# A GRU recurrence followed by a routed spline: the spline's program moves into the recurrence's block, and the last tile's work changes its order

## The chip, the cores and the metric

The kernel runs on one core of one Trainium2 chip. The metric is the device time of one execution in microseconds, median of three. Times inside an execution are counted from the start of the span, which runs from the first instruction to the last.

## What is computed

The reference, cut to what matters:

```python
xs = jnp.swapaxes(inputs, 0, 1)                  # a GRU over 1024 steps, batch 4, width 1024
_, hs = jax.lax.scan(cell, initial_state, xs)
xn = layernorm(hs) * ln_gamma + ln_beta          # 4096 tokens of 1024
...                                              # signs of xn choose one of 64 experts for each token
x_slice = 16 consecutive elements of xn, those of the token's expert
mn, mx = least and greatest element of x_slice over all tokens of the same expert
u = clip((x_slice - mn) / (mx - mn + 1e-8), 0, 1 - 1e-6)
gi = (u * 16) as an integer
delta = (bases[expert, j, gi] + slopes[expert, j, gi] * local) * output_scale[expert]
y = x + hs + delta, which is added at the 16 elements only
```

The extremes of an expert need all the tokens. So the last part, the spline, can start only when the last tile of tokens has been routed.

## The kernel before, in words

The program is a row of blocks. In a block each engine has an instruction stream of its own; at the end of a block every engine executes a DRAIN and waits in a barrier for the others (these instructions bear the line of the `with nc.Block()`: 145, 566, 1399). The third block, at line 566, holds the recurrence, the fourth, at line 1399, the spline.

The recurrence works in tiles of 128 tokens (two time steps of 64 chains); there are 32. While tile i is computed, the tile before is normalised and the tile before that is routed. For one tile this goes: SP loads the states (`h_tok`, L1226); ScalarE sums and squares them (`act_sum`, `act_squares`, L725 to L731); GpSimd makes `rstd` and `shift` (`pool_scale`, L1099 to L1103); ScalarE normalises (`act_normalise`, L735); VectorE applies gamma and beta (`dve_signed`, L893, L895); ScalarE takes the signs (L740); VectorE scores the experts (`dve_route`, L910 to L922), which gives `hit` and `tile_id`; GpSimd keeps them and gathers the token's 16 elements (`pool_keep`, L1115 to L1124, a DMA that GpSimd issues), then copies them (`pool_pick`, L1131). GpSimd also issues, for each tile, the DMA that adds the states to y (`pool_add`, L1110). The extremes are gathered in three batches, `dve_ends(p, batch, part)`: batch 1 is 12 tiles, batch 2 the last two. Part 0 (L949 to L956) needs the picks, part 1 (L958 to L960) makes `miss`, parts 2 and 3 (L962 to L968) fold into `ends`.

The helper `passes` writes each engine's program as: the body once; a wait for `flag`; a load of `flag` into a register (L559); a branch that skips a second copy of the body with a loop around it. With these inputs the branch is taken on every engine. SP waits at L1340 for the last `pool_add` (`y_added`).

The spline: TensorE turns `ends` (L1404) and then computes `curves(0)`, 12 matmuls that look up the curves of the first four tiles (L1413). VectorE reduces the turned ends and splits them into `row_parts` (L1442 to L1445, with L404 to L408 as helper); TensorE looks up each token's extremes (`per_token`, L1420); VectorE computes the cells (L1457 to L1474) and chooses among curves (`choose`, L1484 to L1490). For each group of three or four tiles GpSimd then issues one indirect DMA for a tile, 32 in all (L1503), which add `delta` to y; it waits for all of them at the end.

Of the kernel before, what the change touches and what calls it, by code (L numbers as in the profile page):

```python
# [13 lines left out]
P = 128  # L14
# [396 lines left out]
def recurrence(nc, ctx, t, h0, gi_dram, sums_dram, states_dram, hs_dram, x_rows, y_rows, tables, late_w):  # L411
# [3 lines left out]

    def pb(name, shape, dt=F32):
        return ctx.enter_context(nc.psum_tensor(name, shape, dt))
# [73 lines left out]

    rz_bank = [pb(f"rz_bank{s}", [P, 512]) for s in range(SETS)]
    n_bank = [pb(f"n_bank{s}", [P, 512]) for s in range(SETS)]
    hit_bank = pb("hit_bank", [P, 512])
    misc_bank = pb("misc_bank", [P, 512])
    affine = pb("affine", [P, TILES, 2 * SLICE])
    affine_banks = affine[:].rearrange("p i f -> p (i f)")
    late_acc = [hit_bank[:], misc_bank[:], affine_banks[:, 0:512], affine_banks[:, 512:1024]]
# [67 lines left out]
    with nc.Block() as block:  # L566
# [75 lines left out]
        def _(pe):  # L642
# [43 lines left out]
            passes(pe, one_pass)  # L686

        def act_step(act, it, u, s, turns, mode=FULL, after_gates=None, after_tanh=None):
            n = steps_to(it, u)
            if mode == DIFFS:  # L690
                act.wait_ge(rz_done[s], n)
                nc.scalar.activation(rz[:, s], rz_bank[s][:], ACT.Sigmoid, scale=UNSCALE).then_inc(rz_ready[s], 1)
# [130 lines left out]
        def dve_step(dve, it, u, s, seeds, mode=FULL, after_sums=None, after_old=None):  # L823
# [7 lines left out]
            else:  # L831
                dve.wait_ge(rz_done[s], n)
                dve.wait_ge(gi_loaded[s][u], it * 64 + 64)
                nc.vector.scalar_tensor_tensor(out=sums[:, s, 0:RZ], in0=rz_bank[s][:], scalar=UNSCALE, in1=gi[:, s, u, 0:RZ],  # L834
# [136 lines left out]
        def _(dve):  # L971
# [50 lines left out]
            def one_pass(p, first):  # L1022
# [71 lines left out]
            passes(dve, one_pass)  # L1094

# [38 lines left out]
        def _(pool):  # L1134
# [22 lines left out]
            def one_pass(p, first):  # L1157
# [190 lines left out]
def spline(nc, ctx, t, y_slices):  # L1348

    def sb(name, shape, dt=F32):  # L1350
        return ctx.enter_context(nc.sbuf_tensor(name, shape, dt))
# [33 lines left out]
    tok_bank = ctx.enter_context(nc.psum_tensor("tok_bank", [P, 512], F32))  # L1385
    turn_bank = tok_bank[0:NT, 4 * TILES:4 * TILES + 2 * P]
    curve_bank = ctx.enter_context(nc.psum_tensor("curve_bank", [P, 7, 512], F32))
# [3 lines left out]
    math_step, delta_ready, added = (sem(n) for n in ("math_step", "delta_ready", "added"))  # L1391
# [7 lines left out]
    with nc.Block() as block:  # L1399

        @block.tensor
        def _(pe):
            for e in range(2):
                ins = nc.tensor.transpose(turn_bank[:, e * P:(e + 1) * P], t["ends"][:, e], t["ident"][:])  # L1404
            ins.then_inc(ends_turned, 1)

            def curves(g):
                if g >= 2:
                    pe.wait_ge(curve_used, g - 1)
                a, b = GROUPS[g]  # L1410
                for i in range(a, b):
                    for part in range(3):
                        ins = nc.tensor.matmul(curve_bank[:, 4 * (g % 2) + i - a], hits_t[:, i], curve_parts[:, part],  # L1413
                                               start=part == 0, stop=part == 2)
                ins.then_inc(curve_ready, 1)

            def per_token(a, b):
                for i in range(a, b):
                    for part in range(3):
                        ins = nc.tensor.matmul(tok_bank[:, i * 4:(i + 1) * 4], hits_t[:, i], row_parts[:, part],  # L1420
                                               start=part == 0, stop=part == 2)
                ins.then_inc(tok_ready, 1)

            curves(0)
            pe.wait_ge(rows_split, 1)
            per_token(*CELLS[0])
            pe.wait_ge(tok_known, 1)
            per_token(CELLS[0][1], TILES)
            for g in range(1, len(GROUPS)):
                curves(g)  # L1430

        @block.vector
        def _(dve):
            done = [0]

            def step(ins):
                done[0] += 1
                ins.then_inc(math_step, 1)
                dve.wait_ge(math_step, done[0])

            dve.wait_ge(ends_turned, 1)
            step(nc.vector.tensor_reduce(rows[:, ROW_EXT:ROW_EXT + 1], turn_bank[:, 0:P], AX.X, ALU.min))  # L1442
            step(nc.vector.tensor_reduce(rows[:, ROW_EXT + 1:ROW], turn_bank[:, P:2 * P], AX.X, ALU.max))
            split_exactly(nc.vector, dve, [row_parts[:, i] for i in range(3)], [row_left[:, i] for i in range(2)],
                          rows[:, ROW_SCALE:ROW], step).then_inc(rows_split, 1)  # L1445

            def wide(ap):
                return ap.rearrange("p (i o) -> p i o", o=1).broadcast_to([P, ap.shape[1], SLICE])

            def cells(n):  # L1450
                a, b = CELLS[n]
                s = slice(a, b)
                scale, tile_id, low, high = (per_tok[:, s, f] for f in range(4))
                if n < 2:
                    known = slice(a, TILES if n else b)
                    dve.wait_ge(tok_ready, n + 1)
                    nc.vector.tensor_copy(per_tok[:, known], tok_bank[:, 4 * a:4 * known.stop].rearrange("p (i f) -> p i f", f=4))                      .then_inc(tok_known, 1)  # L1457
                    dve.wait_ge(tok_known, n + 1)
                step(nc.vector.tensor_tensor(span[:, s], high, low, ALU.subtract))
                step(nc.vector.tensor_scalar(span_eps[:, s], span[:, s], 1e-8, None, ALU.add))  # L1460
                step(nc.vector.tensor_tensor(off[:, s], records[:, s], wide(low), ALU.subtract))  # L1461
                step(nc.vector.reciprocal(rspan[:, s], span_eps[:, s]))
                step(nc.vector.tensor_tensor(u_raw[:, s], off[:, s], wide(rspan[:, s]), ALU.mult))  # L1463
                step(nc.vector.tensor_scalar(u_clip[:, s], u_raw[:, s], 0.0, 1.0 - 1e-6, ALU.max, ALU.min))  # L1464
                step(nc.vector.tensor_scalar(u_grid[:, s], u_clip[:, s], float(GRID), None, ALU.mult))  # L1465

                step(nc.vector.tensor_copy(near_i[:, s], u_grid[:, s]))  # L1467
                step(nc.vector.tensor_copy(near[:, s], near_i[:, s]))  # L1468
                step(nc.vector.tensor_tensor(above[:, s], near[:, s], u_grid[:, s], ALU.is_gt))  # L1469
                step(nc.vector.tensor_tensor(cell[:, s], near[:, s], above[:, s], ALU.subtract))  # L1470
                step(nc.vector.tensor_copy(cell_i[:, s], cell[:, s]))  # L1471
                for k, half in enumerate(HALVES):
                    nc.vector.tensor_scalar(in_upper[:, k, s], cell_i[:, s], half, None, ALU.bitwise_and)  # L1473
                step(nc.vector.tensor_tensor(local[:, s], u_grid[:, s], cell[:, s], ALU.subtract))  # L1474

            def choose(g):

                a, b = GROUPS[g]
                s = slice(a, b)
                curve = curves_of(g)  # L1480
                dve.wait_ge(curve_ready, g + 1)
                for k, half in enumerate(HALVES):
                    upper = in_upper[:, k, s].rearrange("p i j -> p (i j)").rearrange("p (m c g) -> p m c g", c=1, g=1)
                    step(nc.vector.copy_predicated(curve[:, :, :, 0:half], upper.broadcast_to([P, (b - a) * SLICE, 2, half]),  # L1484
                                                   curve[:, :, :, half:2 * half]))
                base, slope = (curve[:, :, c, 0].rearrange("p (i j) -> p i j", j=SLICE) for c in range(2))
# [5 lines left out]
            for n, (a, b) in enumerate(CELLS):  # L1492
                cells(n)
                for g, (first, last) in enumerate(GROUPS):
                    if a <= first < b:
                        choose(g)
# [121 lines left out]
```

## Time and profile before

| what | value |
|---|---|
| median of three runs | 2510.69 us (2509.69 to 2511.22) |
| profiled execution, its own time | 2510.37 us |
| its span | 2508.6 us |
| TensorE busy | 2354.8 us (94%) |
| VectorE busy | 1301.2 us (52%) |
| ScalarE busy | 661.4 us (26%) |
| GpSimd busy | 190.5 us (8%) |
| mean granted TensorE clock | 0.965 |

The profiled execution takes 1.8 us more than its span. TensorE's share is an average over three stages: the last 110 us or so, where the last tile is finished and the spline runs, look quite different from the rest. A profile reader should look at that tail by its timeline, with the instructions of the sequencers (load, branch, drain) that do not count as busy.

### The profile page before, as it was taken

How to read it: one execution, taken by the hardware profiler on the slowest of the kernel's cores; microseconds unless marked ns; L12 is line 12 of the kernel's file. 1: busy time of each engine (PE TensorE's matmuls, PEld its weight loads, DVE VectorE, ACT ScalarE, POOL GpSimd, SP SyncE). 2: the span in 40 equal slices, each digit the busy share in tenths (PEclk: the TensorE clock that was granted, in tenths of full speed). 3: DMA queues.
4: the chain of work that ended last, by engine and by line, in shares of the span. 5: the costliest groups of instructions: out<-in, count | busy, mean ns of one | idle time of the engine just before them, and what ended most of it. 6: DMA issues, size and time to landing. Idle time of an engine off the chain costs nothing. (4 is left out here: it accounts for less than half of the span.)

```text
span 2508.6 us, 83678 instructions
## 1 busy us (share of the span) xinstructions
PE 2354.8 (94%) x35300; PEld 1294.4 (52%) x35300; DVE 1301.2 (52%) x2682; ACT 661.4 (26%) x1333; POOL 190.5 (8%) x376
## 2 busy tenths in 40 slices
PE   7999999999999989999999999999999999977734
PEld 3444444444444444555666666666666666544411
DVE  4322121212123357676666655666666666888865
ACT  2200000000001223333333333333333333355510
POOL 0000000000000000000000000111111111122217
PEclk9999999999999999999999999999999999999955
DMA  6594131313132455443444444444444444477712
GB/s 213 166 345 163 51 126 51 126 52 129 51 143 101 151 156 153 138 150 116 136 135 135 135 127 111 118 117 117 117 116 117 115 116 119 128 228 233 219 43 4
DMA packets 179894, 330.33 MB, mean 132 GB/s; under 512 B 27856, under 2 KB 89728, under 8 KB 178752
## 3 DMA queue, kind: packets, MB, share of 16 engines
q1 hardware_dynamic: 145360, 267.53, 33.7%
q10 hardware_dynamic: 24192, 44.05, 4.7%
q0 software_dynamic: 10240, 17.31, 4.7%
q8 instruction: 75, 1.23, 0.2%
q14 instruction: 27, 0.22, 0.0%
HBM read 222.13 MB, written 156.77 MB: 151 GB/s over the span
## 5 line engine op out<-in xcount | busy, mean ns | idle before, releaser
L573 PE MATMUL rz_bank<-w_hi,hi 128*32 128x512 f16 x6912 | 422.7, 387 | 52.9 <-DVE hi L869 36.7
L308 DVE SCALAR_TENSOR_TENSOR out_stage<-acc,bias_row 128x512 f32<-128x512 f32 x168 | 116.2, 691 | 629.0 <-PE acc L364 629.0
L362 PE MATMUL acc<-w_hi,x_even 128*128 128x512 f16 x768 | 293.3, 382 | 17.8 <-DVE x_even L300 11.3
L573 PEld LDWEIGHTS rz_bank<-w_hi,hi 128*32 128x32 f16 x6912 | 177.9, 98 | 231.6 <-DVE hi L869 44.8
L363 PE MATMUL acc<-w_hi,x_even 128*128 128x512 f16 x768 | 293.1, 382 | 0.0
L364 PE MATMUL acc<-w_lo,x_even 128*128 128x512 f16 x768 | 292.9, 381 | 0.0
L696 ACT ACTIVATE rz<-sums 128x512 f32<-128x512 f32 x176 | 111.1, 631 | 541.2 <-DVE sums L834 540.9
L834 DVE SCALAR_TENSOR_TENSOR sums<-rz_bank,stage 128x512 f32<-128x512 f32 x176 | 121.5, 690 | 244.9 <-PE rz_bank L573 244.8
L573 PE MATMUL rz_bank<-w_lo,hi 128*32 128x512 f16 x4096 | 243.4, 379 | 0.0
L573 PE MATMUL rz_bank<-w_hi,lo 128*32 128x512 f16 x4096 | 243.4, 379 | 0.0
L573 PE MATMUL n_bank<-w_hi,hi 128*32 128x256 f16 x6912 | 234.8, 279 | 0.0
L573 PEld LDWEIGHTS n_bank<-w_hi,hi 128*32 128x32 f16 x6912 | 191.3, 100 | 55.5 <-issue 5.9
L362 PE MATMUL acc<-w_hi,x_keep 128*128 128x512 f16 x576 | 218.3, 379 | 0.4 <-issue 0.4
L363 PE MATMUL acc<-w_hi,x_keep 128*128 128x512 f16 x576 | 218.3, 379 | 0.0
L364 PE MATMUL acc<-w_lo,x_keep 128*128 128x512 f16 x576 | 218.3, 379 | 0.0
L573 PEld LDWEIGHTS rz_bank<-w_hi,lo 128*32 128x32 f16 x4096 | 111.2, 97 | 82.7
L573 PEld LDWEIGHTS rz_bank<-w_lo,hi 128*32 128x32 f16 x4096 | 111.1, 97 | 82.8 <-issue 0.2
L701 ACT ACTIVATE n_act<-n_sum 128x256 f32<-128x256 f32 x216 | 90.3, 418 | 179.0 <-DVE n_sum L847 178.3
L573 PE MATMUL n_bank<-w_hi,lo 128*32 128x256 f16 x4096 | 134.2, 273 | 0.0
L573 PE MATMUL n_bank<-w_lo,hi 128*32 128x256 f16 x4096 | 134.2, 273 | 0.0
L362 PEld LDWEIGHTS acc<-w_hi,x_even 128*128 128x128 f16 x768 | 75.5, 98 | 109.9 <-issue 13.6
L573 PEld LDWEIGHTS n_bank<-w_hi,lo 128*32 128x32 f16 x4096 | 110.2, 97 | 28.9
(191 smaller groups left out, 2665.3 us busy)
## 6 DMA issues: line engine op xcount, KB each, us to landing
stage<-gi_scratch SPq DMA_DIRECT2D x704, 96.0 KB
gi_scratch<-out_stage ACTq DMA_DIRECT2D x168, 256.0 KB, 2.0
stage<-sums_scratch SPq DMA_DIRECT2D x40, 512.0 KB
stage<-in_xT SPq DMA_DIRECT2D x32, 512.0 KB, 6.4
y<-in_x_rows SPq DMA_DIRECT2D x32, 512.0 KB, 4.4
hs_scratch<-h SPq DMA_DIRECT2D x128, 128.0 KB
x_keep<-hs_scratch SPq DMA_DIRECT2D x32, 512.0 KB, 3.9
y<-hs_scratch POOLq DMA_DIRECT2D x32, 512.0 KB
```

The lines of the kernel that those rows point to most:

```text
L308: nc.vector.scalar_tensor_tensor(out=out_stage[:, tb], in0=acc[e % BANKS][:], scalar=UNSCALE, in1=bias_row[:].rearrange("p q f -> p (q f)" ...
L362: nc.tensor.matmul(acc[e % BANKS][:], hi, wh, start=k == 0, stop=False)
L363: nc.tensor.matmul(acc[e % BANKS][:], lo, wh, start=False, stop=False)
L364: last = nc.tensor.matmul(acc[e % BANKS][:], hi, wl, start=False, stop=k == KB - 1)
L573: last = nc.tensor.matmul(bank[q * COLS:(q + 1) * COLS, 0:b - a], state[:, s, j], w[:, j, q * QW + a:q * QW + b], start=first and j == 0, ...
L696: nc.scalar.activation(rz[:, s], sums[:, s, 0:RZ], ACT.Sigmoid).then_inc(rz_ready[s], 1)
L701: nc.scalar.activation(n_act[:, s], n_sum[:, s], ACT.Tanh).then_inc(n_ready[s], 1)
L834: nc.vector.scalar_tensor_tensor(out=sums[:, s, 0:RZ], in0=rz_bank[s][:], scalar=UNSCALE, in1=gi[:, s, u, 0:RZ], op0=ALU.mult, op1=ALU.add ...
```

## The change

The spline no longer has a block of its own. `spline()` returns three functions, for TensorE, VectorE and GpSimd, and the recurrence calls each behind `passes` in the same block. In them `curves(0)` comes ahead of the turning of `ends`; a semaphore `ends_ready`, which VectorE increments at the start of its part, stands where the barrier stood. The PSUM banks are one tensor for both parts, and the spline's scratch lies in the room of `w_lo`. GpSimd waits for `y_added` as well, behind its last pick. The loop over tiles on GpSimd ends one tile earlier and the last turn is written out: keep, scale, add, pick, where it was add, keep, scale, pick. On VectorE part 1 of batch 1 comes ahead of `dve_signed`.

```diff
@@ def one_pass (VectorE)
                 nc.vector.tensor_copy(flag[:], misc_bank[0:1, 64:65]).then_inc(pass_judged, 1)
+                dve_ends(dve, p, 1, 1)
                 dve_signed(dve, T)
-                dve_ends(dve, p, 1, 1)
                 dve_route(dve, T)
@@
             passes(dve, one_pass)
+            dve_spline(dve)
@@ def one_pass (GpSimd)
-                with pool.Fori(2, TILES + 1) as i:
+                with pool.Fori(2, TILES) as i:
                     tile(i, True)
+                T = p * TILES + TILES
+                pool_keep(pool, T - 1, TILES - 2)
+                pool_scale(pool, T, TILES - 1)
+                pool_add(pool, T, TILES - 1)
+                pool_pick(pool, T - 1, TILES - 2)
                 pool_keep(pool, p * TILES + TILES, TILES - 1)
                 pool_pick(pool, p * TILES + TILES, TILES - 1)
+                pool.wait_ge(y_added, p * (TILES * 16) + TILES * 16)
+                pool.sem_inc(wait_carrier, 1)
 
             passes(pool, one_pass)
+            pool_spline(pool)
@@ spline
-    with nc.Block() as block:
-        @block.tensor
-        def _(pe):
-            for e in range(2):
-                ins = nc.tensor.transpose(turn_bank[:, e * P:(e + 1) * P], t["ends"][:, e], t["ident"][:])
-            ins.then_inc(ends_turned, 1)
...
-            curves(0)
-            pe.wait_ge(rows_split, 1)
+    def pe_spline(pe):
...
+        curves(0)
+        pe.wait_ge(ends_ready, 1)
+        for e in range(2):
+            ins = nc.tensor.transpose(turn_bank[:, e * P:(e + 1) * P], t["ends"][:, e], t["ident"][:])
+        ins.then_inc(ends_turned, 1)
+        pe.wait_ge(rows_split, 1)
...
+    def dve_spline(dve):
...
+        dve.sem_inc(ends_ready, 1)
+        dve.wait_ge(ends_turned, 1)
```

## Rows read from the trace of the kernel before

**Rows 1.** The page, busy time of each engine over the whole span.

```profile
PE 2354.8 (94%) x35300; PEld 1294.4 (52%) x35300; DVE 1301.2 (52%) x2682; ACT 661.4 (26%) x1333; POOL 190.5 (8%) x376
```

**Rows 2.** The chain that ended last, in order of time: start, us, what.

```profile
2429.90 0.61 PE tok_bank L1404 x2
2430.50 5.23 PE curve_bank L1413 x12
2435.73 0.31 PE tok_bank L1420 x12
...
2436.07 0.19 DVE per_tok L1457
...
2502.42 1.55 POOL y L1503
```

**Rows 3.** The timeline from 2398 to 2444 us: start, us, engine, line, idle time before.

```profile
2398.27 0.08 DVE L922 DVE_READ_ACCUMULATOR late_out<-late_out,best,tile_ids 128x1 f32 x1
...
2400.48 1.00 POOL L1110 DMA_DIRECT2D y<-hs_scratch  x1 [11.16 <-DMA x_keep<-hs_scratch]
...
2402.13 0.19 ACT L731 ACTIVATION_READ_ACCUMULATOR x_keep<-x_keep,neg_mean 128x1 f32 x1
...
2403.08 1.11 POOL L1124 DMA_INDIRECT late_out<-hs_scratch,row_now  x1 [0.71 <-ACT x_keep L731]
2404.26 0.19 POOL L1099 TENSOR_SCALAR var_eps<-square_sum 128x1 f32<-128x1 f32 x1
...
2405.59 1.24 ACT L735 ACTIVATE x_keep<-x_keep,shift,rstd 128x1024 f32<-128x1024 f32 x1 [3.27 <-POOL shift L1103]
...
2406.86 1.23 DVE L893 TENSOR_TENSOR x_keep<-x_keep,gamma_s 128x1024 f32<-128x1024 f32 x1 [3.14 <-ACT x_keep L735]
...
2409.26 0.55 DVE L958 TENSOR_SCALAR late_out<-bias_row 128x768 f32<-128x768 bf16 x1
2409.38 1.06 ACT L740 ACTIVATE bias_row<-x_keep 128x1024 bf16<-128x1024 f32 x1 [2.39 <-DVE x_keep L895]
...
2411.84 1.22 DVE L910 TENSOR_REDUCE late_out<-bias_row 128x64 f32<-128x1024 bf16 x1
...
2420.36 0.19 DVE L949 TENSOR_TENSOR late_out<-picks,rstd 128x32 f32<-128x32 f32 x1 [0.45 <-POOL picks L1131]
...
2424.31 0.23 DVE L968 TENSOR_TENSOR ends<-late_out,ends 128x64 f32<-128x64 f32 x1
...
2431.94 0.16 DVE L408 CAST row_parts<-row_left 64x4 bf16<-64x4 f32 x1
...
2443.57 1.65 POOL L1503 DMA_INDIRECT y<-delta,row_i  x1 [23.40 <-DVE delta L1490]
```

**Rows 4.** Line 559, load of the flag and branch: ns min/median/max, first and last start.

```profile
L559 PEldq COMPARE_BRANCH  x1: 3698/3698/3698, 2416.4 to 2416.4; - x1
...
L559 DVEq TENSOR_LOAD <-flag x1: 548/548/548, 2424.7 to 2424.7; - x1
...
L559 DVEq COMPARE_BRANCH  x1: 56/56/56, 2426.0 to 2426.0; - x1
```

**Rows 5.** Line 566, the end of the recurrence's block.

```profile
L566 POOLq DRAIN  x1: 5297/5297/5297, 2421.0 to 2421.0; - x1
L566 DVEq DRAIN  x1: 77/77/77, 2429.5 to 2429.5; - x1
```

**Rows 6.** Line 1399, the end of the spline's block.

```profile
L1399 POOLq DRAIN  x1: 2660/2660/2660, 2505.7 to 2505.7; - x1
```

**Rows 7.** Line 145, the end of the second block.

```profile
L145 POOLq DRAIN  x1: 41/41/41, 3.3 to 3.3; - x1
```

**Rows 8.** The three lines on which GpSimd issues DMAs, each asked for alone.

```profile
L1110 POOL DMA_DIRECT2D y<-hs_scratch x32: 894/992/1101, 1528.7 to 2400.5; - x32
L1124 POOL DMA_INDIRECT late_out<-hs_scratch,row_now x32: 1081/1102/1177, 1572.9 to 2416.1; - x32
L1503 POOL DMA_INDIRECT y<-delta,row_i x32: 1545/1554/1653, 2443.6 to 2502.4; - x32
```

More of the change, by code:

```diff
@@ L1 @@
+import math
 import concourse.bass as bass
@@ L490, in recurrence @@
     rstd, shift, hits_t = t["rstd"], t["shift"], t["hits_t"]
[L492 to L498, printed above, removed]
+    banks = t["banks"]
+    rz_bank = [banks[:, s] for s in range(SETS)]
+    n_bank = [banks[:, SETS + s] for s in range(SETS)]
+    hit_bank, misc_bank = banks[:, 4], banks[:, 5]
+    affine = banks[:, 6:8].rearrange("p b f -> p (b f)").rearrange("p (i f) -> p i f", f=2 * SLICE)
+    late_acc = [banks[:, 4 + tb] for tb in range(TB)]
     gi_loaded = t["gi_loaded"]
@@ L1348, in spline @@
 def spline(nc, ctx, t, y_slices):
+    room = t["w_lo"][:].rearrange("p k n -> p (k n)")
+    taken = [0]
     def sb(name, shape, dt=F32):
-        return ctx.enter_context(nc.sbuf_tensor(name, shape, dt))
+        halves = math.prod(shape[1:]) * (1 if dt == BF16 else 2)
+        flat = room[0:shape[0], taken[0]:taken[0] + halves].bitcast(dt)
+        taken[0] += (halves + 15) // 16 * 16
+        dims = "abc"[:len(shape) - 1]
+        return flat.rearrange(f"p ({' '.join(dims)}) -> p {' '.join(dims)}", **dict(zip(dims, shape[1:])))
     def sem(name):
@@ L1384, in spline @@
     CELLS = ((0, 4), (4, 18), (18, TILES))
-    tok_bank = ctx.enter_context(nc.psum_tensor("tok_bank", [P, 512], F32))
+    tok_bank = t["banks"][:, 7]
     turn_bank = tok_bank[0:NT, 4 * TILES:4 * TILES + 2 * P]
-    curve_bank = ctx.enter_context(nc.psum_tensor("curve_bank", [P, 7, 512], F32))
+    curve_bank = t["banks"][:, 0:7]
     ends_turned, row_step, rows_split, tok_ready, tok_known, curve_ready, curve_used = (
         sem(n) for n in ("ends_turned", "row_step", "rows_split2", "tok_ready", "tok_known", "curve_ready", "curve_used"))
-    math_step, delta_ready, added = (sem(n) for n in ("math_step", "delta_ready", "added"))
+    math_step, delta_ready, added, ends_ready = (sem(n) for n in ("math_step", "delta_ready", "added", "ends_ready"))
     def curves_of(g):
@@ L1397, in curves_of @@
         return curve_bank[:, first:first + b - a].rearrange("p i (j c g) -> p (i j) c g", c=2, g=GRID)
-    with nc.Block() as block:
-        @block.tensor
-        def _(pe):
-            for e in range(2):
-                ins = nc.tensor.transpose(turn_bank[:, e * P:(e + 1) * P], t["ends"][:, e], t["ident"][:])
-            ins.then_inc(ends_turned, 1)
[L1407 to L1422, printed above, removed]
-            curves(0)
-            pe.wait_ge(rows_split, 1)
[L1426 to L1486, printed above, removed]
-                step(nc.vector.tensor_tensor(rise[:, s], slope, local[:, s], ALU.mult))
-                nc.vector.tensor_tensor(value[:, s], base, rise[:, s], ALU.add).then_inc(curve_used, 1)
-                dve.wait_ge(curve_used, g + 1)
-                nc.vector.tensor_tensor(delta[:, s], value[:, s], wide(per_tok[:, s, 0]), ALU.mult).then_inc(delta_ready, 1)
[L1492 to L1496, printed above, removed]
-        @block.gpsimd
-        def _(pool):
-            for g, (a, b) in enumerate(GROUPS):
-                pool.wait_ge(delta_ready, g + 1)
-                for i in range(a, b):
-                    pool.indirect_dma_start(out=y_slices[:], out_offset=bass.IndirectOffsetOnAxis(ap=row_i[:, i:i + 1], axis=0),
-                                            in_=delta[:, i], in_offset=None, compute_op=ALU.add).then_inc(added, 16)
-            pool.wait_ge(added, 16 * TILES)
@@ new lines, in pe_spline, with curves, per_token @@
+    def pe_spline(pe):
+        def curves(g):
+            if g >= 2:
+                pe.wait_ge(curve_used, g - 1)
+            a, b = GROUPS[g]
+            for i in range(a, b):
+                for part in range(3):
+                    ins = nc.tensor.matmul(curve_bank[:, 4 * (g % 2) + i - a], hits_t[:, i], curve_parts[:, part],
+                                           start=part == 0, stop=part == 2)
+            ins.then_inc(curve_ready, 1)
+        def per_token(a, b):
+            for i in range(a, b):
+                for part in range(3):
+                    ins = nc.tensor.matmul(tok_bank[:, i * 4:(i + 1) * 4], hits_t[:, i], row_parts[:, part],
+                                           start=part == 0, stop=part == 2)
+            ins.then_inc(tok_ready, 1)
+        curves(0)
[4 more added lines that the diff above has]
+        pe.wait_ge(rows_split, 1)
+        per_token(*CELLS[0])
+        pe.wait_ge(tok_known, 1)
+        per_token(CELLS[0][1], TILES)
+        for g in range(1, len(GROUPS)):
+            curves(g)
@@ new lines, in dve_spline, with step, wide, cells @@
+    def dve_spline(dve):
+        done = [0]
+        def step(ins):
+            done[0] += 1
+            ins.then_inc(math_step, 1)
+            dve.wait_ge(math_step, done[0])
+        dve.sem_inc(ends_ready, 1)
+        dve.wait_ge(ends_turned, 1)
+        step(nc.vector.tensor_reduce(rows[:, ROW_EXT:ROW_EXT + 1], turn_bank[:, 0:P], AX.X, ALU.min))
+        step(nc.vector.tensor_reduce(rows[:, ROW_EXT + 1:ROW], turn_bank[:, P:2 * P], AX.X, ALU.max))
+        split_exactly(nc.vector, dve, [row_parts[:, i] for i in range(3)], [row_left[:, i] for i in range(2)],
+                      rows[:, ROW_SCALE:ROW], step).then_inc(rows_split, 1)
+        def wide(ap):
+            return ap.rearrange("p (i o) -> p i o", o=1).broadcast_to([P, ap.shape[1], SLICE])
+        def cells(n):
+            a, b = CELLS[n]
+            s = slice(a, b)
+            scale, tile_id, low, high = (per_tok[:, s, f] for f in range(4))
+            if n < 2:
+                known = slice(a, TILES if n else b)
+                dve.wait_ge(tok_ready, n + 1)
+                nc.vector.tensor_copy(per_tok[:, known], tok_bank[:, 4 * a:4 * known.stop].rearrange("p (i f) -> p i f", f=4))                      .then_inc(tok_known, 1)
+                dve.wait_ge(tok_known, n + 1)
+            step(nc.vector.tensor_tensor(span[:, s], high, low, ALU.subtract))
+            step(nc.vector.tensor_scalar(span_eps[:, s], span[:, s], 1e-8, None, ALU.add))
+            step(nc.vector.tensor_tensor(off[:, s], records[:, s], wide(low), ALU.subtract))
+            step(nc.vector.reciprocal(rspan[:, s], span_eps[:, s]))
+            step(nc.vector.tensor_tensor(u_raw[:, s], off[:, s], wide(rspan[:, s]), ALU.mult))
+            step(nc.vector.tensor_scalar(u_clip[:, s], u_raw[:, s], 0.0, 1.0 - 1e-6, ALU.max, ALU.min))
+            step(nc.vector.tensor_scalar(u_grid[:, s], u_clip[:, s], float(GRID), None, ALU.mult))
+            step(nc.vector.tensor_copy(near_i[:, s], u_grid[:, s]))
+            step(nc.vector.tensor_copy(near[:, s], near_i[:, s]))
+            step(nc.vector.tensor_tensor(above[:, s], near[:, s], u_grid[:, s], ALU.is_gt))
+            step(nc.vector.tensor_tensor(cell[:, s], near[:, s], above[:, s], ALU.subtract))
+            step(nc.vector.tensor_copy(cell_i[:, s], cell[:, s]))
+            for k, half in enumerate(HALVES):
+                nc.vector.tensor_scalar(in_upper[:, k, s], cell_i[:, s], half, None, ALU.bitwise_and)
+            step(nc.vector.tensor_tensor(local[:, s], u_grid[:, s], cell[:, s], ALU.subtract))
+        def choose(g):
+            a, b = GROUPS[g]
+            s = slice(a, b)
+            curve = curves_of(g)
+            dve.wait_ge(curve_ready, g + 1)
+            for k, half in enumerate(HALVES):
+                upper = in_upper[:, k, s].rearrange("p i j -> p (i j)").rearrange("p (m c g) -> p m c g", c=1, g=1)
+                step(nc.vector.copy_predicated(curve[:, :, :, 0:half], upper.broadcast_to([P, (b - a) * SLICE, 2, half]),
+                                               curve[:, :, :, half:2 * half]))
+            base, slope = (curve[:, :, c, 0].rearrange("p (i j) -> p i j", j=SLICE) for c in range(2))
+            step(nc.vector.tensor_tensor(rise[:, s], slope, local[:, s], ALU.mult))
+            nc.vector.tensor_tensor(value[:, s], base, rise[:, s], ALU.add).then_inc(curve_used, 1)
+            dve.wait_ge(curve_used, g + 1)
+            nc.vector.tensor_tensor(delta[:, s], value[:, s], wide(per_tok[:, s, 0]), ALU.mult).then_inc(delta_ready, 1)
+        for n, (a, b) in enumerate(CELLS):
+            cells(n)
+            for g, (first, last) in enumerate(GROUPS):
+                if a <= first < b:
+                    choose(g)
@@ L1508, in constants, with pool_spline @@
+    def pool_spline(pool):
+        for g, (a, b) in enumerate(GROUPS):
+            pool.wait_ge(delta_ready, g + 1)
+            for i in range(a, b):
+                pool.indirect_dma_start(out=y_slices[:], out_offset=bass.IndirectOffsetOnAxis(ap=row_i[:, i:i + 1], axis=0),
+                                        in_=delta[:, i], in_offset=None, compute_op=ALU.add).then_inc(added, 16)
+        pool.wait_ge(added, 16 * TILES)
+    return pe_spline, dve_spline, pool_spline
 def constants(nc, t):
```

14 lines of the change are left out of this document (6 added, 8 removed).

## The prediction

> **What bounds the kernel now.** I read the page first. TensorE is busy 94% of the span [rows 1], but that is the recurrence, which the change leaves alone: no instruction of its loops is added, removed or moved, apart from GpSimd's last turn. So I looked at the end. The chain in order of time [rows 2] shows what sets it from 2430 us on: the two transposes, `curves(0)` for 5.23 us, `per_token`, VectorE's cells, and then GpSimd's indirect DMAs, the last of which is issued at 2502.42. The reader is to see that the first `curves(0)` stands between the transposes and `per_token`. Then I read the timeline of the 30 us ahead of it, to follow the last tile from engine to engine [rows 3], and last the sequencers' own instructions at lines 559, 566, 1399 and 145 [rows 4 to 7], since a barrier and a branch are not busy time and the timeline leaves them out. All of 2398 to 2508 us is one thread of short waits, so a microsecond saved in it comes off the end, unless something takes it back behind it.
>
> **The last tile's order.** Two moves, of which both must hold for the gain.
>
> GpSimd: before, it waits for the states' load, issues `pool_add` at 2400.48, keeps, issues the gather at 2403.08 (1.11 us), and only at 2404.26 starts `pool_scale`, though the sum of squares was there at 2402.13 + 0.19 = 2402.32 [rows 3]. After, keep needs only `tile_id`, there at 2398.35 (2398.27 + 0.08), and can start then. From 2400.48 to the end of the gather's issue at 2404.19 it took 3.7 us with the add inside, 2.7 without it. So GpSimd is free at about 2401.1 and scale starts near 2402.45, when it is the squares that come last. Scale takes 2405.59 - 2404.26 = 1.33 us to ScalarE's start, so `xhat` starts at 2403.8 and is done at 2405.0, against 2406.83: 1.8 us earlier. `pool_add` comes behind it with 1.0 us of GpSimd; the pick, the next keep and SP's wait stand behind it, and the next keep is not due for 7 us.
>
> VectorE: the flag is copied at 2406.86 - 3.14 = 2403.72, then it idles until `xhat`. Part 1 of batch 1 takes 2411.84 - 2409.26 = 2.58 us and fits from 2403.74 to 2406.3. `dve_signed` then starts at 2406.3; it takes 2.49 us (2406.86 to 2409.35), ScalarE's signs 1.06 and two handovers of 0.03. Routing starts at 2409.9 against 2411.84 [rows 3]: **1.9 us saved**. The cover is gone that part 1 gave to the signs: VectorE now idles 1.1 us there, which is counted in it. Had GpSimd's part gained nothing, `dve_signed` would start at 2406.86 still and 1.4 us would be left. Behind routing the order stands: keep, gather, pick, with parts 2 and 3 beside them, which leave 0.45 us of idle before L949 in both. So `ends` are finished at 2424.54 - 1.9 = 2422.6. The lower bound of this term is 1.4, the upper 2.0.
>
> **The barrier.** From the end of `ends` at 2424.54 to the transposes at 2429.90 lie 5.3 us, and the idle time looks like the barrier's. It isn't. VectorE loads the flag at 2424.7 (0.55 us), reaches its branch at 2426.0, and its first instruction behind the branch, the DRAIN, is at 2429.5 [rows 4, 5]; TensorE's branch took 3.7 us in the same way. The code to be skipped is as long after the change, VectorE's `ends_ready` stands behind the same branch, and it is TensorE that waits for it. So 5.0 of the 5.3 us stay. What goes is the barrier's own handshake, 2429.5 to 2429.9; a semaphore of about 0.15 us takes its place. **0.2 us saved**, between 0 and 0.35.
>
> **`curves(0)` ahead.** TensorE's branch at 2416.4 lands 3.7 us later [rows 4], at 2418.2 with the 1.9 taken off; 5.2 us of `curves(0)` end at 2423.5, where `ends_ready` comes at 2427.6. So it lies under VectorE's branch with 4 us to spare. If that cover were gone it would cost up to 5.2. Then `row_parts`, done at 2432.10 (2431.94 + 0.16), let `per_token` start at once. Its 12 small matmuls added 0.31 us behind a full TensorE, and two transposes took 0.61 from a standstill [rows 2]; I take 0.55 for them and 0.1 for the handover. The copy that stood at 2436.07 would stand at 2432.75: **3.3 us saved**, between 3.2 and 3.6. From `per_token` on every distance is as before: cells, choose, first scatter 7.5 us later, 32 scatters. GpSimd's added wait for `y_added` is met by 2410 or so, while it would scatter at 2438.1.
>
> Sum so far: 1.9 + 0.2 + 3.3 = 5.4 us. The last scatter is issued at 2497.0 and landed at 2500.1, not 2505.5.
>
> **The DRAIN at the end.** This is where I expect the gain to go. GpSimd's DRAIN at the end of the recurrence took 5.30 us, from 2421.0 to 2426.3, under VectorE's branch, so that nobody waited for it [rows 5]. Its DRAIN at the end of the spline took 2.66 us, and it ends the span [rows 6]. Neither waits for a transfer: the pick had landed before the first, and the second stands behind the wait for all 32 scatters. Where GpSimd had issued no DMA, the DRAIN took 0.04 us [rows 7]. Now count: 32 adds and 32 gathers stand ahead of the first DRAIN, 32 scatters ahead of the second [rows 8]. 5.297 / 64 is 0.083 us for a DMA; 2.660 / 32 is 0.083 us. I read it as work that GpSimd owes for each DMA it has issued since the last DRAIN. With one block there is one DRAIN, behind all 96: 96 x 0.083 = 7.96 us, at the end, where nothing covers it. That is **5.3 us lost**. Any cost that adds up over DMAs gives the same, whatever share each kind has. The bounds: 0 if the length doesn't go by what was issued (then 2.66 stays), 5.3 if it adds up. I take 5.3, because two rows and the empty one lie on a line through nothing.
>
> The Trainium skill, VectorE: DVE Perf Modes, section "The DRAIN you can't avoid", calls the DRAINs that surround a kernel boilerplate of a constant 12 ns or so on all engines. By that page the merged DRAIN would cost nothing more, and the time would be 2505.3. These rows (5.297 and 2.660 us on GpSimd) already speak against it here.
>
> **The sum** against the profiled execution (2510.37 us, its span of 2508.6 and 1.8 around it): 2510.37 - 5.4 + 5.3 = 2510.3. The median of the runs, 2510.69, is 0.3 above the profiled one; against it I get 2510.6 and take **2510.5 us**.
>
> **Rivals.**
>
> 1. The DRAIN is no longer than before (2.66 us), be it constant or reset in another way. For it: a DRAIN that starts after all has landed has nothing obvious to do. Against it: rows 5 to 7. It gives 2510.7 - 5.4 = 2505.3 us, faster by 0.21%, just over the bound.
> 2. The DRAIN's debt has a ceiling, at the 64 DMAs seen: 5.3 us in place of 2.66. For it: nothing longer was seen. Against it: nothing shows a ceiling either. It gives 2510.7 - 5.4 + 2.6 = 2507.9.
> 3. Slower: the debt grows faster than the count when 96 DMAs stand before one DRAIN. The place is the same last DRAIN. To make the kernel slower by 0.2% (5.0 us) it must take 2.66 + 5.4 + 5.0 = 13.1 us, or 0.136 us for a DMA; at 0.15 the DRAIN is 14.4 and the time 2517.0. Against it: from 32 to 64 the price for one stayed 0.083.
> 4. The order doesn't do what it says: VectorE still waits for `xhat`, or the gather lands later. Then up to 1.9 us of the gain are missing, and with the DRAIN of 7.96 the time is 2512.4, still within the bound.
>
> A measurement of this kernel can tell about 0.2%, 5.0 us, from no change.
>
> **How the numbers follow.** Chances: my forecast 0.64; rival 1 0.16; rival 2 0.08; rival 3 0.04; rival 4 0.08. Rival 1 lies on the edge of the bound, so about two thirds of it count as faster, and a few hundredths for gains I missed: faster 0.13. Slower is rival 3 and a little for what I don't see: 0.05. The rest, 0.82, is within. The range takes in the forecast, rivals 2 and 4 and the spread of the runs shown (1.5 us): 2507.0 to 2512.8. It leaves out rivals 1 and 3, which hold 2 in 10.
>
> **What would show it.** In the profile after: routing of the last tile starts about 1.9 us earlier relative to the load of the states; `ends` to transposes stays near 5.1 us, with some 3.5 of it behind VectorE's branch; `curves(0)` ends some 4 us before the transposes; `per_token` follows `row_parts` in 0.1 us; the last scatter is issued near 2497.0. The step that decides is the one GpSimd DRAIN at the end of line 566: near 8.0 us by my reading, 2.7 by rival 1, 5.3 by rival 2. The prediction is wrong if that DRAIN is short, or if VectorE's branch lands sooner when no barrier stands behind it, which would give up to 3.5 us more.

## The result, and the profile after

The kernel after takes 2506.91 us (median of 20 runs, 2505.1 to 2509.56) against 2510.61 us before (20 runs): 3.7 us less, a ratio of 0.9984 with a 95% interval of 0.9977 to 0.9991. I had said 2510.5 us, 2507.0 to 2512.8. So the time moved where I had forecast no change that could be told, and it lies just under my range. The profiled execution took 2506.94 us, its span 2505.4 us against 2508.6.

First the timeline after, for the stretch of [rows 3]: the last tile.

```profile
2399.85 1.07 POOL L1124 DMA_INDIRECT late_out<-hs_scratch,row_now  x1 [0.57 <-issue]
...
2402.49 0.18 POOL L1099 TENSOR_SCALAR var_eps<-square_sum 128x1 f32<-128x1 f32 x1 [1.57 <-ACT x_keep L730]
...
2403.57 0.54 DVE L957 TENSOR_SCALAR late_out<-bias_row 128x768 f32<-128x768 bf16 x1
2403.64 1.24 ACT L734 ACTIVATE x_keep<-x_keep,shift,rstd 128x1024 f32<-128x1024 f32 x1 [1.34 <-POOL shift L1103]
2404.00 1.01 POOL L1110 DMA_DIRECT2D y<-hs_scratch  x1 [0.40 <-issue]
...
2406.16 1.23 DVE L892 TENSOR_TENSOR x_keep<-x_keep,gamma_s 128x1024 f32<-128x1024 f32 x1
...
2409.77 1.22 DVE L909 TENSOR_REDUCE late_out<-bias_row 128x64 f32<-128x1024 bf16 x1 [1.12 <-ACT bias_row L739]
...
2418.21 5.30 PE L1421 MATMUL banks<-curve_parts,late_ring 64*128 64x512 bf16 x12 [4.60 <-issue]
...
2422.33 0.22 DVE L967 TENSOR_TENSOR ends<-late_out,ends 128x64 f32<-128x64 f32 x1
...
2437.93 1.62 POOL L1514 DMA_INDIRECT y<-w_lo,row_i  x1 [19.74 <-DVE w_lo L1502]
```

GpSimd's scale now waits for ScalarE's squares (1.57 us idle ahead of L1099), where before the squares had lain ready from 2402.32 until GpSimd took them up at 2404.26. `miss` (L957) starts at once behind the flag, and `signed` (L892) behind it without idle time. Routing (L909) starts at 2409.77 against 2411.84 [rows 3]. `curves(0)` (L1421) is done at 2423.5, well ahead of the turning of `ends`.

The chain in order of time, for the stretch of [rows 2]:

```profile
2424.00 0.06 DVEq L557
2424.05 3.50 issue
2427.56 0.03 DVEq L1452
2427.59 0.04 issue
2427.63 0.65 PE banks L1435 x2
...
2429.93 0.49 PE banks L1428 x12
2430.44 0.18 DVE w_lo L1469
```

With the barrier gone the profile names what [rows 4, 5] showed between the lines: from VectorE's branch (line 557 now) to its next instruction, the increment of `ends_ready` (L1452), 3.50 us pass in which it waits for nothing that the profile shows. Then the turning of `ends` and `per_token` follow at once.

And the end of the block (line 564 now), which answers to [rows 5, 6]:

```profile
L564 POOLq DRAIN  x1: 5338/5338/5338, 2499.8 to 2499.8; - x1
```

That is the surprise. The one DRAIN behind 96 DMAs takes 5.34 us: more than the 2.66 before, less than the 7.96 that I had added up.

### The profile page after: what moved, and what is told of

It is laid out like the page before. It is cut to its first block and busy times, and to the rows that moved or that the text cites. A ratio compares the mean times of both kernels' runs of the same rounds, so it can differ in the third digit from the quotient of the medians.

```text
span 2505.4 us, 83655 instructions
## 1 busy us (share of the span) xinstructions
PE 2339.9 (93%) x35300; PEld 1288.7 (51%) x35300; DVE 1299.7 (52%) x2682; ACT 660.6 (26%) x1333; POOL 189.4 (8%) x376
## 5 line engine op out<-in xcount | busy, mean ns | idle before, releaser
L571 PE MATMUL banks<-w_hi,hi 128*32 128x512 f16 (+1 forms) x13824 | 605.1, 328 | 61.4 <-DVE hi L868 45.3
L571 PEld LDWEIGHTS banks<-w_hi,hi 128*32 128x32 f16 x13824 | 363.3, 97 | 288.3 <-DVE hi L868 56.2
L571 PE MATMUL banks<-w_hi,lo 128*32 128x512 f16 (+1 forms) x8192 | 355.2, 326 | 0.0
L571 PE MATMUL banks<-w_lo,hi 128*32 128x512 f16 (+1 forms) x8192 | 355.2, 326 | 0.0
L571 PEld LDWEIGHTS banks<-w_lo,hi 128*32 128x32 f16 x8192 | 221.3, 97 | 111.7
L571 PEld LDWEIGHTS banks<-w_hi,lo 128*32 128x32 f16 x8192 | 221.2, 97 | 111.7
L833 DVE SCALAR_TENSOR_TENSOR sums<-banks,stage 128x512 f32<-128x512 f32 x176 | 121.3, 689 | 247.6 <-PE banks L571 247.5
L364 PEld LDWEIGHTS acc<-w_hi,x_even 128*128 128x128 f16 x768 | 75.5, 98 | 109.6 <-issue 12.9
L366 PEld LDWEIGHTS acc<-w_lo,x_even 128*128 128x128 f16 x768 | 75.5, 98 | 91.8 <-issue 2.1
L365 PEld LDWEIGHTS acc<-w_hi,x_even 128*128 128x128 f16 x768 | 75.5, 98 | 91.3 <-issue 1.7
L858 DVE TENSOR_TENSOR n_sum<-not_z,n_act 128x256 f32<-128x256 f32 x216 | 91.5, 423 | 36.9 <-ACT n_act L700 36.9
```

Source lines behind the costliest of these rows:

```text
L364: nc.tensor.matmul(acc[e % BANKS][:], hi, wh, start=k == 0, stop=False)
L365: nc.tensor.matmul(acc[e % BANKS][:], lo, wh, start=False, stop=False)
L366: last = nc.tensor.matmul(acc[e % BANKS][:], hi, wl, start=False, stop=k == KB - 1)
L571: last = nc.tensor.matmul(bank[q * COLS:(q + 1) * COLS, 0:b - a], state[:, s, j], w[:, j, q * QW + a:q * QW + b], start=first and j == 0, ...
L858: nc.vector.tensor_tensor(new_n[:, s], not_z[:, s], n_act[:, s], ALU.mult).then_inc(new_n_ready[s], 1)
```

## The experiments

All medians stand against the kernel before on the same chip (2510.57 us, 2510.87 for the second set, which is experiments 2 and 7 to 9, and one run of 2510.19 in experiment 3). The time of one kernel varies by 4 to 6 us from run to run (2509.14 to 2514.53 before, 2505.10 to 2509.56 after). In the profiled runs of the kernels with the new order the last tile but one is kept on GpSimd (L1115 in the kernel after) anywhere from 2396.95 to 2403.07 us, so much of this lies ahead of the tail. So I read a small part from distances inside the tail.

**1. What a DRAIN of GpSimd costs.** A kernel of blocks. In each, GpSimd issues n DMAs of one kind, waits for them (every 32, and at the end), and the block ends:

```python
for i in range(n):
    issue(pool, kind, i, sem)
    if i % 32 == 31:
        pool.wait_ge(sem, 16 * (i + 1))
pool.wait_ge(sem, 16 * n)
```

> A kernel of blocks in which only GpSimd issues DMAs, waits for all of them, and ends the block with its DRAIN; it computes nothing of the reference. Theory 1 (bookkeeping of 0.083 us for each DMA since the last DRAIN, with a ceiling at about 64): gathers of 128 rows, 8, 16, 32, 48, 64, 80, 96 and 128 of them, give DRAINs of 0.7, 1.3, 2.7, 4.0, 5.3, 5.3, 5.3 and 5.3 us; 32, 64 and 96 scatters 2.7, 5.3 and 5.3; 32 adds of 128 KB, 32 loads and 32 tiny loads of one row 2.7 each, 96 of them 5.3; one tiny load 0.1. Theory 2 (the work goes by descriptors, and the ceiling is that of a descriptor ring): tiny loads of one row give far less than gathers of 128 rows, 32 tiny ones under 0.5 us, 96 of them about three times as much, with no ceiling there. Theory 3 (the adds and the gathers of the recurrence cost, and the scatters beside them do not, or the other way): gathers and scatters of the same number give different DRAINs, and each kind grows in a straight line with its number.

Measured, the GpSimd row of each block's line:

```profile
L59 POOLq DRAIN  x1: 2655/2655/2655, 133.0 to 133.0; - x1
...
L63 POOLq DRAIN  x1: 5268/5268/5268, 287.2 to 287.2; - x1
...
L67 POOLq DRAIN  x1: 7882/7882/7882, 529.7 to 529.7; - x1
...
L69 POOLq DRAIN  x1: 1262/1262/1262, 707.3 to 707.3; - x1
...
L71 POOLq DRAIN  x1: 2655/2655/2655, 770.4 to 770.4; - x1
...
L73 POOLq DRAIN  x1: 2817/2817/2817, 897.2 to 897.2; - x1
...
L75 POOLq DRAIN  x1: 5432/5432/5432, 1084.8 to 1084.8; - x1
...
L85 POOLq DRAIN  x1: 7877/7877/7877, 1279.8 to 1279.8; - x1
```

These are 32, 64, 96 and 128 gathers, then 32, 64 and 96 scatters, and last 96 loads of 64 bytes. 8, 16, 48 and 80 gathers gave 0.72, 1.35, 3.96 and 6.57 us; 32 adds 2.66, 32 loads 2.65, one load of 64 bytes 0.12. From 8 to 96 gathers the DRAIN rises by (7.882 - 0.719) / 88 = 0.081 us for each, and 96 loads of one row cost the same as 96 gathers of 128 rows. So the price goes by the number of DMAs and not by their kind, size or descriptors, and with that theories 2 and 3 fall as to the price. But the ceiling of theory 1 falls too: 96 gathers cost 7.9 us. Instead the length drops: 128 gathers leave the debt of about 15, 64 scatters that of 34, 96 scatters that of 66. I call what is owed for one DMA an entry, and read the drop as entries that were cleared before the DRAIN came. The timeline shows a place for it, where an issue waits for nothing that the profile shows and yet comes late:

```profile
687.11 0.95 POOL L20 DMA_INDIRECT room<-in_x,rows  x1 [3.13 <-issue]
...
888.28 1.55 POOL L23 DMA_INDIRECT y<-room,rows  x1 [1.78 <-issue]
```

The first is the 114th of the 128 gathers, the second the 61st of the 64 scatters; elsewhere this idle time is 0.30 us. When the clearing comes does depend on the kind.

**2. The same with the recurrence's own mixture**, 32 adds of 512 KB and 32 gathers in turn, and then 0 to 64 scatters.

> A kernel of blocks in which only GpSimd issues DMAs and ends each with its DRAIN; it computes nothing of the reference. Each of the first eight begins as the recurrence does (32 adds of 512 KB and 32 gathers in turn, each waited for) and goes on with 0, 4, 8, 12, 16, 24, 32 and 64 scatters. Theory A (an entry is owed for every DMA, 0.082 us each in the DRAIN, and when some store of them is full, entries are cleared in the stream of issues): the DRAIN rises by 0.082 us for each scatter from 5.3 us, falls by about 2.5 us (31 entries) at one number of scatters between 4 and 32, where the interval between two issues is longer by 1 to 1.5 us, and stands at 5.3 us again with 32 scatters. Theory B (a ceiling of 64 or 65 entries): 5.3 us for every number of scatters, with no drop and no long interval. In the blocks of one kind theory A expects: 48 scatters 4.0, 62 scatters 2.7, 112 gathers 9.2, 120 gathers 0.6 to 0.7; theory B expects nothing of the kind, as the first ladder already had 7.9 us for 96 gathers.

```profile
L61 POOLq DRAIN  x1: 5290/5290/5290, 315.2 to 315.2; - x1
...
L65 POOLq DRAIN  x1: 5926/5926/5926, 878.2 to 878.2; - x1
...
L67 POOLq DRAIN  x1: 3190/3190/3190, 1171.5 to 1171.5; - x1
...
L73 POOLq DRAIN  x1: 4823/4823/4823, 2113.0 to 2113.0; - x1
```

These are the blocks with 0, 8, 12 and 32 scatters. Between 8 and 12 the DRAIN falls by 2.7 us, where four more DMAs should add 0.3: some 37 entries went (3.06 us at 0.082 for each). The timeline of the block with 12 scatters shows the place, ahead of the last one:

```profile
1162.98 1.56 POOL L28 DMA_INDIRECT y<-room,rows  x1 [0.30 <-issue]
1164.85 1.56 POOL L28 DMA_INDIRECT y<-room,rows  x1 [0.30 <-issue]
1168.27 1.56 POOL L28 DMA_INDIRECT y<-room,rows  x1 [1.86 <-issue]
```

The idle time ahead of an issue is 1.86 us in place of 0.30. The blocks with 16, 24 and 32 scatters (3.52, 4.17 and 4.82 us) have the long idle time in the same place, ahead of the 76th DMA (1.84 to 1.88 us), and the blocks with 0, 4 and 8 have none. So theory A holds in its course up to 32 scatters: a rise of 0.08 for each, one drop, and a longer interval there; theory B, a ceiling, would have shown neither. Its numbers held less well: with 32 scatters I expected 5.3 us and got 4.8. In the blocks of one kind 48 and 62 scatters gave 3.96 and 2.66 us, 112 and 120 gathers 9.19 and 0.61, all as expected.

The blocks for which nothing was expected show that no single count sets the clearing. 64 scatters behind the mixture give 2.82 us, with long idle times ahead of the 76th and again the 114th DMA. 128 and 192 scatters (0.98 and 3.76 us) have them ahead of the 61st, the 114th and the 121st, and 192 also ahead of the 181st. 192 gathers (6.59 us) have one, ahead of the 114th; 192 loads of 64 bytes (5.27 us) have one of 4.52 us, ahead of the 129th; 32 gathers and 32 scatters in turn (5.27 us) have none.

**3. Where in the kernel after the entries go.** Three kernels with one more DRAIN, behind the 4th, 11th or 25th scatter. The edit of the first; the others have `i == 10` and `i == 24`:

```diff
                                         in_=delta[:, i], in_offset=None, compute_op=ALU.add).then_inc(added, 16)
+                if i == 3:
+                    pool.drain()
```

> The kernel after with one more DRAIN on GpSimd behind the 4th of the 32 scatters, where it waits for the second group in any case. It asks how many entries stand after 68 DMAs. With 0.0817 us for each entry and 0.05 on top: 68 entries give 5.6 us; if the 31 that are missing at the end (65 stand there and not 96) were cleared by then, 37 entries give 3.1. The last DRAIN then has 28 entries, 2.3 us.

> The same behind the 11th scatter, 75 DMAs in: 6.2 us if all 75 stand, 3.6 if 31 were cleared by then (the ladder with the same mixture cleared about 37 between the 75th and the 76th DMA, so 6.2 is the likelier). The last DRAIN has 21 entries, 1.8 us. Both DRAINs take about 0.25 us for the start as well, and the scatters behind it are later by its length.

> The same behind the 25th scatter, 89 DMAs in: 7.3 us if the clearing comes only at the very end, 4.8 if it came between the 12th and the 25th, as in the ladder. The last DRAIN has 7 entries, 0.6 us.

The rows of the three added DRAINs:

```profile
L1517 POOLq DRAIN  x1: 13085/13085/13085, 2436.2 to 2436.2; - x1
...
L1517 POOLq DRAIN  x1: 15710/15710/15710, 2452.2 to 2452.2; - x1
...
L1517 POOLq DRAIN  x1: 19922/19922/19922, 2468.8 to 2468.8; - x1
```

The first begins at 2436.2, ahead of the first scatter (2436.45), though it stands behind the 4th: such a row holds more than the DRAIN's work. So I count from the end of the issue ahead of it to its end. The first ends at 2449.30, and the issue ahead of it ended at 2443.66: 5.6 us, all 68 entries. Behind the 11th scatter the same distance is 6.2 us, all 75. Behind the 25th it is 5.0 us, and 89 entries would be 7.3: some 28 had gone. The last DRAINs, with 28, 21 and 7 scatters behind, took 2.34, 1.76 and 0.62 us, as expected. So in the kernel, too, entries are cleared on the way, behind the 11th scatter and by the 25th. What stays open: no interval in that stretch is longer by 1.5 us as it was in experiment 2 (from the first to the last issue 58.79 us pass in the kernel after, with the clearing, and as many in the kernel of experiment 4, whose last DRAIN shows none); why some 28 had gone at the 25th scatter and 31 at the end; and why 37 went in experiment 2. One time each was taken: 2508.01, 2512.63 and 2506.17 us, too few to rank these kernels. But a DRAIN between scatters is in their way: the idle time ahead of the next issue is 6.72, 6.93 and 5.76 us, where it was 1.31, 0.30 and 0.30.

**4. A DRAIN under cover.** The kernel after with one more DRAIN where GpSimd has nothing to do:

```diff
             passes(pool, one_pass)
+            pool.drain()
             pool_spline(pool)
```

> The kernel after, with one more DRAIN on GpSimd, behind the last pick and the flag's branch and ahead of the scatters. If the last DRAIN is long because of the 64 DMAs of the recurrence (theories 1 and 2), the new one takes 5.3 us from about 2419.2 to 2424.5, under VectorE's branch and ahead of the first scatter at 2437.9, and the last one falls from 5.34 to 2.66 us: span 2.7 us shorter than the kernel after, 2504.2 us against 2506.9. If the last DRAIN has a length that does not go by what was issued, it stays at 5.3 and so does the time, 2506.9.

```profile
L564 POOLq DRAIN  x1: 2660/2660/2660, 2499.7 to 2499.7; - x1
L1182 POOLq DRAIN  x1: 5297/5297/5297, 2418.9 to 2418.9; - x1
```

2504.89 us (10 runs), ratio 0.9978 (0.9968 to 0.9987); the span of the profiled run is 2502.6 us, 2.8 less than after. (The medians differ by 2.0 us and their intervals overlap, so the rows and the span carry this reading.) The second row is the new one, at 2418.9 to 2424.2, and the first scatter comes at 2437.7 as before. The merge had moved 5.30 us of covered DRAIN to the end, the clearing took 2.6 of it back, and this takes back the rest.

**5. The order alone.** The kernel before with the new order of GpSimd and VectorE in the last tile.

```diff
+                dve_ends(dve, p, 1, 1)
                 dve_signed(dve, T)
-                dve_ends(dve, p, 1, 1)
...
-                with pool.Fori(2, TILES + 1) as i:
+                with pool.Fori(2, TILES) as i:
                     tile(i, True)
+                T = p * TILES + TILES
+                pool_keep(pool, T - 1, TILES - 2)
+                pool_scale(pool, T, TILES - 1)
+                pool_add(pool, T, TILES - 1)
+                pool_pick(pool, T - 1, TILES - 2)
```

> The kernel before with the new order of the last tile alone (GpSimd keeps and scales ahead of the add, VectorE makes miss ahead of signed). By the profile after, this part is worth 2.0 us: the last routing starts 2.0 us earlier and the span ends 2.0 us earlier, 2508.6 us against 2510.6; the two DRAINs stay 5.3 and 2.66. If the merged block makes the order pay only in part, under 1 us is seen here.

2507.93 us (11 runs), ratio 0.9988 (0.9979 to 0.9997), the span 2506.7 us, 1.9 less than before. Routing starts at 2409.56, and `ends` are finished at 2422.45. The order pays its whole share without the merge.

**6. The first curves behind the turning again.** The kernel after, with

```diff
-        curves(0)
         pe.wait_ge(ends_ready, 1)
...
         ins.then_inc(ends_turned, 1)
+        curves(0)
         pe.wait_ge(rows_split, 1)
```

> The kernel after with the first curves behind the turning of ends again, and all else of the change. By my reading (5.3 us of curves that lay under VectorE's branch come back between the transposes and per_token, of which 1.7 lie under VectorE's reductions) the time is 3.3 us longer than after, 2510.2 us. If the barrier was what the change removed (rival), moving the curves back costs under 1 us and the time stays under 2508.

2511.57 us (11 runs), ratio to before 0.9999 (0.9990 to 1.0008). From the start of turning to the copy of the tokens' values:

```profile
2432.42 0.64 PE L1434 MATMUL banks<-ident,ends 128*64 128x128 f32 x2 [14.06 <-DVEq L1452]
2432.99 5.30 PE L1421 MATMUL banks<-curve_parts,late_ring 64*128 64x512 bf16 x12
...
2438.62 0.17 DVE L1469 COPY w_lo<-banks 128x16 f32<-128x16 f32 x1 [3.97 <-PE banks L1428]
```

It is 6.2 us, as before the change (2429.90 to 2436.07) [rows 2], against 2.8 after: 3.4 us. The median is longer than after by 4.7 us, 1.3 more than that, and the cause of the 1.3 is not shown. The profiled run is no help with it: it was the slowest of the eleven (2515.21 us), and its whole tail starts 4.7 us late (GpSimd's keep at 2403.07 against 2398.36).

**7. What the 5 us between `ends` and the turning are.** The kernel after with only the first pass in `passes`, on all engines:

```diff
         eng.sem_inc(wait_carrier, 1)
-        with eng.If(eng.value_load(flag[0:1, 0:1], min_val=0, max_val=P) > 0):
-            with eng.Fori(1, CHUNKS + 1) as p:
...
```

> The kernel after without the flag's load and branch and without the second copy of the body, on all engines. With these inputs the copy is skipped anyway; the text of the reference that needs it (more passes over the recurrence) is left out. By my reading the 5.3 us between the end of ends and the turning of ends are the load of the flag and the fetch behind the branch: they fall to about 0.2 us, unless curves(0), which would then start near 2413.8 and end at 2419.1, or anything else is later; span 5.1 us shorter than after, 2501.8 us. If the time is spent in handing over between the parts of the block (rival), it stays near 2506.9. With no code to skip the fetches at 2414.4 to 2418.2 on TensorE go as well.

```profile
2420.94 0.23 DVE L961 TENSOR_TENSOR ends<-late_out,ends 128x64 f32<-128x64 f32 x1
...
2421.41 0.64 PE L1429 MATMUL banks<-ident,ends 128*64 128x128 f32 x2 [3.77 <-DVEq L1446]
```

It is 0.24 us in place of 5.1. The time is 2501.5 us (8 runs), ratio 0.9970 (0.9960 to 0.9980). Load, test and branch, with the code that they skip, are nearly all of it.

**8. The spline ahead of the skipped code.** This keeps the second copy, but TensorE and VectorE reach the spline without a jump over it:

```diff
+        again = eng.value_load(flag[0:1, 0:1], min_val=0, max_val=P)
+        if not late:
+            with eng.If(again < 1):
+                tail(eng)
+        with eng.If(again > 0):
             with eng.Fori(1, CHUNKS + 1) as p:
...
+            if not late:
+                tail(eng)
+        if late:
+            tail(eng)
```

`tail` is the engine's part of the spline; `late` is set for GpSimd, whose branch is hidden.

> The kernel after with the spline's code on TensorE and VectorE placed ahead of the second copy of the body, under its own test of the flag, so that the usual way falls through without a jump over the copy; the copy is followed by a spline of its own. The load of the flag stays (1.3 us to the branch), the fetch (3.5 us on VectorE) goes: ends to the turning of ends 1.8 to 2.0 us in place of 5.3, time 3.3 us shorter than after, 2503.6 us. If the wait behind the branch is not the jump's, the time stays at 2506.9.

The time is 2503.37 us (9 runs), ratio 0.9971 (0.9961 to 0.9981). `ends` are done at 2425.65 in its profiled run, and the turning starts at 2427.26: 1.6 us, of which 0.55 are the load. 3.5 us of 5.1 were the jump. The Trainium skill, Runtime: NRT & Kernel Launch, section "Instruction fetch mechanics", says that a taken branch whose target is outside the two pages at hand stalls for a fetch. The trace agrees as far as it goes: 3.50 us behind VectorE's branch, gone when the usual way falls through. How far the target lies it does not show. A branch alone does not cost this: in the kernel after, ScalarE's next instruction comes 0.5 us behind its branch at the same line, SP's 2.6 us, and in experiment 4 GpSimd's 0.2 us.

**9. All together.** Experiment 8, the DRAIN of experiment 4, and a third one ahead of the last wait, so that the debt of the scatters is paid while the last of them land:

```diff
+            def drained(pool):
+                pool.drain()
+                pool_spline(pool)
...
+        pool.drain()
         pool.wait_ge(added, 16 * TILES)
```

> The kernel after with the spline's code first, a DRAIN on GpSimd behind the last pick, and another behind the issue of the last scatter and ahead of the wait for all of them. From the second 2.7 us, from the first 3.3 us; the third overlaps the 1.5 us in which the last scatters land, so that 2.66 us of DRAIN stand from the last issue and the one at the end of the block takes under 0.1 us: 1.5 us more. Sum 7.5 us less than after, 2499.4 us. If the DRAIN ahead of the wait must itself wait until all has landed, the last part gives nothing: 2500.9 us.

```profile
L572 POOLq DRAIN  x1: 52/52/52, 2497.6 to 2497.6; - x1
L1189 POOLq DRAIN  x1: 5297/5297/5297, 2418.9 to 2418.9; - x1
L1526 POOLq DRAIN  x1: 21627/21627/21627, 2475.7 to 2475.7; - x1
```

2499.52 us (5 runs), ratio 0.9959 (0.9946 to 0.9973): it beats both kernels, the one before by 11.4 us. The block's own DRAIN is down to 0.05 us. The row of the third (L1526) begins at 2475.7 and ends at 2497.36; the last issue ended at 2494.57. That is 2.8 us. In the kernel after, 1.5 us pass between the last issue and the block's DRAIN, in which the scatters land; had the DRAIN to wait for them, the distance would be some 4.2 us. So its work overlaps the landing.

## Why the prediction was wrong

**Step by step.** The gain ahead of the DRAIN was put at 5.4 us and measured 5.7: the last scatter is issued at 2496.72 against 2502.42. The two profiled runs can be laid side by side here: the next to last tile is scored at 2398.28 us after and at 2398.35 before.

- *The last tile's order, 1.9 us:* `ends` are finished at 2422.55 against 2424.54, 2.0 us. Right, and experiment 5 shows it by itself.
- *The barrier, 0.2 us:* `ends` to turning fell from 5.36 to 5.08 us, 0.3 (the prediction called the 5.36 "5.3"). Right, and for the reason given: experiments 7 and 8 show that the idle time at the barrier was the flag's load and the jump over the second copy.
- *`curves(0)` ahead, 3.3 us:* from turning to the copy of the tokens' values 2.81 us against 6.17, 3.4. Right; undone in experiment 6.
- *The DRAIN at the end, 5.3 us lost:* this is the step that failed. It did grow, and it was the place to look, but to 5.34 us and not to 7.96, so 2.7 us were lost and not 5.3. The price of 0.083 us for a DMA was right (0.081 in experiment 1), and so was "whatever share each kind has". What was wrong is "any cost that adds up over DMAs gives the same", with no term for a clearing on the way: by the length of the DRAIN some 31 of the 96 entries (2.6 us) were gone before it came. With 64 DMAs before the first DRAIN and 32 before the second the trace of before stood below that point, and two rows and an empty one on a line could not show where the line ends. Experiment 2 shows the drop between the 75th and the 76th DMA of this mixture, experiment 3 that the kernel's own comes behind the 75th and before the DRAIN behind the 89th. What triggers it stays open.

**The rivals.** Rival 2, a ceiling at 64, gave 2507.9 us and came closest, 1.0 us off, but by luck: experiment 1 shows 7.9 us behind 96 gathers, so there is no such ceiling; some 31 of 96 had been cleared, which leaves 65. Rival 1, a DRAIN of 2.66 us whatever came before, is refuted by the row of 5.34 us. The same row speaks against the constant of about 12 ns that the prediction cites from the Trainium skill, VectorE: DVE Perf Modes, section "The DRAIN you can't avoid": at the ends of these blocks GpSimd's DRAIN took 0.04 to 5.34 us. Rival 3 did not come: the price for one stayed at 0.08. Nor did rival 4: VectorE found `xhat` ready.

**The sum again** with the measured terms, against the profiled execution: 2510.37 - 5.7 + 2.7 = 2507.4, and 2506.94 was measured. Of the 0.4 us left, 0.2 lie between the end of the last issue and the start of the DRAIN (1.7 us before, 1.5 after) and 0.2 outside the span (1.8 against 1.6). The medians differ by 3.7 us, 0.7 more than the two terms; the runs of one kernel lie 4 to 6 us apart.

**The range** reached 2507.0. With a DRAIN of 5.3 us and a gain of 5.7 the prediction's own sum is 2507.6, which leaves 0.6 us to the bound, less than half of the 1.5 us by which the three runs shown had differed. So the margin around the lowest case was too thin, and that case was in the range for a ceiling that does not exist: the number came near, the mechanism behind it did not.

## What to carry to other kernels

When two blocks become one, look not only at what the barrier cost but at what each engine did in it under another's cover: here GpSimd paid 5.3 us there for its 64 DMAs, and after the merge it paid at the very end. Ask for a DRAIN where the engine idles, and put the last one ahead of the last wait. Read an idle stretch ahead of a barrier by its sequencers' rows: of 5.4 us here, 0.3 were the barrier and 3.5 a jump over code that never runs, which goes when the usual way falls through.

## What the runs showed of the hardware that I had not expected

- GpSimd's DRAIN costs 0.081 us for each DMA that it has issued since the last one and that has not been cleared, from 0.12 us behind one load to 9.19 us behind 112 gathers, though all have landed. A load of 64 bytes counts as much as a gather of 128 rows.
- The debt is cleared in part on the way: behind the 113th gather (120 gathers leave 0.61 us), behind the 60th scatter (62 leave 2.66 us in place of some 5.1), and in the recurrence's mixture between the 75th and the 76th DMA. There the idle time ahead of the next issue is 3.1 to 3.3 us for gathers, 1.8 to 1.9 for scatters and 1.8 to 1.9 for the mixture, in place of 0.30. What it goes by is open; it is not the number alone, and in the kernel after no such idle time is seen.
- A DRAIN ahead of the wait for the last scatters does its work while they land.
